# Two ordering edits on ScalarE and VectorE in a fused two-layer kernel: the first join of the slot softmax, and the activation-table switches of the last rounds

## The reference, cut to what matters

```python
# layer 0: s is self-attention with Q = K = V; g is a soft mixture of 64 experts with 32 slots each
logits = (einsum('tzd,ed->tze', x, phi_w) + phi_b).reshape(t, z, 64, 32)
D = softmax(logits, axis=3); C = softmax(logits, axis=2)
X_tilde = einsum('tznp,tzd->npd', D, x)                  # sums over ALL rows
X_tilde = tanh(layernorm(clip(X_tilde, -33000, 65000)))  # eps 1e-5
Y_tilde = einsum('npd,ndH->npH', X_tilde, expert_w) + expert_b[:, None, :]
Y = einsum('tznp,npH->tzH', C, Y_tilde)
# layer 1: s is a gated linear recurrence over each sequence, RMS-normalised; g a token-mixing FFN
log_a = log(sigmoid(lam) + 1e-8); a_t = exp(8 * r_t * log_a)
gated = sqrt(1 - a_t*a_t + 1e-6) * (i_t * x_proj);  h = a*h + gated   # scan over the sequence
```

## Time and profile before

| what | value |
|---|---|
| time, median of 3 runs | 1244.29 us (1239.99 to 1247.22) |
| the profiled execution's own time | 1247.22 us |
| its span, first to last instruction | 1245.2 us |
| PE busy | 1171.4 us, 94% of the span |
| DVE busy | 1096.9 us, 88% |
| POOL busy | 998.5 us, 80% |
| ACT busy | 865.2 us, 69% |
| mean granted TensorE clock | 0.973 |

### The profile page before, as it was taken

How to read it: one execution, slowest core, us unless ns; L and a number is a source line. 1 busy time by engine, 2 the same in 40 slices (tenths; PEclk the granted TensorE clock), 3 DMA queues, 4 the chain that set the end, 5 groups by cost and what they waited for, 6 DMA issues and landing times. The chain is left out here.

```text
span 1245.2 us, 17223 instructions
## 1 busy us (share of the span) xinstructions
PE 1171.4 (94%) x4994; PEld 776.9 (62%) x4994; DVE 1096.9 (88%) x1596; ACT 865.2 (69%) x1930; POOL 998.5 (80%) x804
## 2 busy tenths in 40 slices
PE   6599999999999999999589999999999999999984
PEld 2366666666666666665267777766777776776751
DVE  6989999999999999999457899889989998999863
ACT  2666666666766666666457887877887787787764
POOL 3499999999999999999478787777788777778720
PEclk9799999999999999999789999999999999999997
DMA  6443334443333344334835343434444343444300
GB/s 192 132 150 124 144 135 151 153 152 134 135 132 147 139 152 152 140 140 147 242 107 160 110 153 104 151 110 136 134 129 140 115 135 128 136 135 129 121 32 17
DMA packets 123214, 167.33 MB, mean 134 GB/s; under 512 B 7153, under 2 KB 99313, under 8 KB 122993
## 3 DMA queue, kind: packets, MB, share of 16 engines
q1 hardware_dynamic: 122688, 164.65, 39.3%
q10 hardware_dynamic: 434, 1.59, 0.4%
HBM read 90.71 MB, written 75.50 MB: 133 GB/s over the span
## 5 line engine op out<-in xcount | busy, mean ns | idle before, releaser
L138 POOL TENSOR_TENSOR exp_slots_loaded<-exp_slots_loaded,slot_max 128x1024 f32<-128x1024 f32 x128 | 332.6, 2620 | 59.3 <-DMA exp_slots_loaded<-exp_slots 58.8
L669 POOL TENSOR_TENSOR dd<-ed,rz 128x512 f32<-128x512 f32 x256 | 265.0, 1052 | 23.8 <-ACT rz L560 23.8
L475 PE MATMUL acc<-dd,xns 128*128 128x512 f32 x512 | 262.3, 594 | 2.4 <-POOL dd L669 1.9
L1346 DVE TENSOR_TENSOR clo<-ct,chi 128x512 fp32r<-128x512 f32 x256 | 172.7, 680 | 53.1 <-ACT chi L1187 51.9
L611 DVE TENSOR_REDUCE mr<-lg 128x16 fp32r<-128x512 f32 x256 | 170.8, 688 | 21.1 <-PE lg L442 17.2
L538 ACT ACTIVATE exp_slots_loaded<-lg 128x512 f32<-128x512 f32 x256 | 145.7, 595 | 55.2 <-PE lg L463 51.5
L680 POOL TENSOR_TENSOR ch<-exp_slots_loaded 128x512 f32<-128x512 f32 x128 | 165.5, 1293 | 12.3 <-ACT exp_slots_loaded L538 12.3
L1187 ACT ACTIVATE chi<-ct 128x512 fp32r<-128x512 f32 x256 | 150.2, 594 | 20.4 <-PE ct L935 19.4
L935 PEld LDWEIGHTS ct<-identity,exp_slots_loaded 128*128 128x128 f32 x1024 | 125.1, 142 | 59.5 <-issue 19.5
L935 PE MATMUL ct<-identity,exp_slots_loaded 128*128 128x128 f32 x1024 | 153.1, 275 | 6.3 <-DVE clo L1346 3.3
L463 PE MATMUL lg<-shift_experts_to_slots,mt 128*128 128x512 f32 x256 | 156.6, 651 | 0.5 <-ACT ed L529 0.5
(11 more groups left out here) (186 smaller groups left out, 2443.7 us busy)
## 6 DMA issues: line engine op xcount, KB each, us to landing
exp_slots<-exp_slots_loaded SPq DMA_DIRECT2D x128, 512.0 KB, 2.8
exp_slots_loaded<-exp_slots SPq DMA_DIRECT2D x128, 512.0 KB, 4.1
xns<-xn_rows SPq DMA_DIRECT2D x128, 64.0 KB, 2.5
expert_w<-in_expert_w SPq DMA_DIRECT2D x8, 512.0 KB, 5.2
b_xraw<-in_xT SPq DMA_DIRECT2D x16, 256.0 KB, 3.8
out_t<-b_ti SPq DMA_DIRECT2D x16, 256.0 KB, 2.1
xn_rows<-slot_max SPq DMA_DIRECT2D x2, 1024.0 KB, 5.1
xn_rows<-slot_sum SPq DMA_DIRECT2D x2, 1024.0 KB, 5.2
```

Source lines behind the costliest of these rows:

```text
L138: e.tensor_tensor(rows, rows, joined(SM, b)[:, h].unsqueeze(2).broadcast_to([P, TPB, GC * EPC, NP]), ALU.mult).then_inc(s_we)
L475: e.matmul(acc[k][:, :], xns[v % RX][:, :], dd[v % RX][:, bank(k)], start=tile == 0, stop=tile == NT - 1, skip_group_check=True).then_inc( ...
L669: e.tensor_tensor(dd[v % RX][:, bank(k)].rearrange("q (n p) -> q n p", p=NP), ed[v % RD][:, bank(k)].rearrange("q (n p) -> q n p", p=NP), ...
L1346: e.tensor_tensor(clo[c % RC][:, :], ct[c % 2][:, :], hi_f32(chi[c % RC][:, :]), ALU.subtract).then_inc(c_l)
```

## The change

The diff has two independent parts. In stage 1b, ScalarE's part of the first join moves from behind its second square to the head of its queue, and VectorE's first part of the join moves from ahead of the four centrings to behind them. In stage 2, the two table preloads are guarded with `within(i)` in place of `i >= 0`. As they are called with i - 1, this takes away the calls of rounds 17 and 18 (arguments 16 and 17), four preloads in all, and leaves those of rounds 1 to 16.

```diff
             def scalar1b(e):
+                join_factors(e, 0)
                 for q in range(4):
                     e.wait_ge(s_ce, q + 1)
                     e.activation(sq[:, bank(q)], xc[:, bank(q)], ACT.Square).then_inc(s_sq)
-                    if q == 1:
-                        join_factors(e, 0)
...
             def vector1b(e):
                 for q in range(4):
                     e.tensor_scalar(XTT[:, bank(q)], XTT[:, bank(q)], -33000.0, 65000.0, ALU.max, ALU.min).then_inc(s_cl)
-                join_max(e, 0)
                 for q in range(4):
                     e.wait_ge(s_me, q + 1)
                     e.tensor_tensor(xc[:, bank(q)], XTT[:, bank(q)], pm[q][:, :], ALU.subtract).then_inc(s_ce)
+                join_max(e, 0)
                 join_inverse(e, 0)
...
                 def log_table(i):
-                    if i >= 0:
+                    if within(i):
                         e.preload_act_table_set("natural_log_exp_and_others")
...
                 def tanh_table(i):
-                    if i >= 0:
+                    if within(i):
                         e.preload_act_table_set("exp_and_others")
```

## The result

The changed kernel takes 1253.44 us in the median of 20 runs, against 1243.69 us of 20 runs of the kernel before. The ratio is 1.0078, with a 95% interval of 1.0054 to 1.0102. It is slower by 9.7 us (6.7 to 12.7). The forecast was no change, at 1244.7 us within 1240.5 to 1252.0, so the time lies outside the range. Rival 1, with 1251.6 us, is the case that came true.

A forecast was written before the change was run, and what follows sets the result against it. TensorE was taken as busy for 94% of the span, with dependent chains in stage 1b and the tail. Stage 1b's +1.7 and the tail's -1.3 us gave +0.4 on the 1244.3 us median: 1244.7 us, range 1240.5 to 1252.

The forecast's parts named there:

- Rival 1: Tail: the compiler's set for Ln lacks Exp, so each alternation costs a load; +7.3 us in all, 1251.6 us, chance 0.25.
- Part 2, the inserted loads: Tail: the compiler reinserts the load at input_log(14) in the removed call's place, cost 0; three loads instead of four.
- The gain of 1.30 us: Round 17: the removed Tanh load ahead of deviation_inverse(15) leaves the chain, its replacement lying in idle time; 1.30 us gained.
- Rival 2: Tail: the load for input_tanh(15) goes behind the wait and is paid in full; +1.7 us, 1246.0 us, chance 0.10.
- Part 1, the relay: Stage 1b: maximum after the last centring, factors 2.34 us later, Ln for lam 3.18 us after them, Tanh 2.3 us later.
- Squares and variances: Stage 1b: squares held behind the factors add nothing; variances done at 612.0, 0.9 us before the fourth deviation Ln.
- Part 1, the end of the stage: Stage 1b: its end moves by +1.7 us, as expert weight loads take 3.7 us instead of 4.4; range 0.7 to 2.3.
- The upper bound of 2.3: End of stage 1b: the full 2.3 us delay is paid if the expert weight loads are no quicker.
- Rival 3: Stage 1b: weight bandwidth alone sets the end, so the 2.3 us vanish; -1.3 us, 1243.0 us, chance 0.10.
- The noise: Whole kernel: comparison noise taken as 0.5%, 6.2 us, so no change to be measured.

The follow-up runs named there:

- e10: The kernel before without the one preload at the head of stage 1 (line 570); 1592.47 us in its one execution.
- e3: The kernel before with only the Tanh preload guarded, the call for Ln and Exp kept in rounds 17 and 18; 1242.87 us, ratio 0.9992.
- e7: The kernel before with the lam job ahead of the join on ScalarE and only the Tanh preload guarded; median 1244.77 us, ratio 0.9997.
- e1: The kernel before with only the two join moves in stage 1b, preloads as before; 1249.1 us, ratio 1.0024.
- e11: The changed kernel with the log_table guard put back to i >= 0, so the Ln and Exp call stands in rounds 17 and 18; ratio 0.9993 to before.
- e2: The kernel before with only the two preload guards, join as before; 1251.13 us, ratio 1.0055.
- e6: The kernel before with only round 18's preloads removed; last sequence's Tanh of y to the span's end 42.27 us, 40.06 before.
- e4: The kernel before with only ScalarE's join move; one execution, last centring to Tanh 7.82 us, 8.50 before.
- e5: The kernel before with only VectorE's join move, the maximum behind the centrings; one execution, last centring to Tanh 10.69 us, 8.50 before.

## Why the prediction was wrong, point by point

- **Part 2, the inserted loads.** This is the step that failed. The prediction said that the load for `input_log(14)` "takes the same place", and put it at 0, which takes for granted that it brings the same set. With it went "Exp is also in the set that is active, so nothing has to be loaded there". The place was right, the set was not: behind each Ln without a preload the next Exp got a load too (1.28 us each), and ten loads stood where three were forecast. Rival 1 named the mechanism, its count comes to the ten loads, and it was sized at 3.0 us in round 17 and 2.6 us in round 18. Measured between the two traces: 3.05 and 2.87, T +5.9. It had 0.25. That the sizes came so near is partly luck. In the kernels whose code there is that of before, the first stretch spreads from 17.83 to 19.02 us (seven kernels, mean 18.34) and the second from 20.92 to 22.23 (six, mean 21.40). Against these means the two kernels with ten loads, 22.07 twice and 23.91 and 24.56, are 3.7 and 2.8 us longer. Stage 1 of e10 shows the same: 257 loads, where the kernel before has one. How the compiler chooses the set, no run shows.
- **The gain of 1.30 us** at `tanh_table` of round 17 needed the set with both to be active. Where it was (e3), the gap between Ln and Exp shrank by 1.29 us. The mechanism was right and its condition wasn't met. A switch costs 1.28 us with 0.01 to 0.02 behind it in all these rows.
- **Rival 2** is half right. The load went behind one of the two waits, the one for the output DMA, but not behind the wait for the gate's product (e3), and so it was not paid in full: nothing in e3, 0.7 us in e7. The earlier trace rows were a poor witness. That activation has two waits as well, and nothing shows whether the load at 2.82 stood behind one of them that had ended early.
- **Part 1, the relay.** Factors to Ln for lam took 608.98 - 605.78 = 3.20 us (3.18 expected). The 0.02 us of issue between the last centring and the maximum is shown by no run. In the changed kernel the maximum started at 604.66, 0.09 us ahead of the centring's recorded end (604.06 + 0.69 = 604.75). From the last centring to Tanh it became 2.32 us longer (2.34 expected). Squares and variances set nothing, as worked out: the variances' passes ended at 606.77 + 5.34 = 612.11 and the fourth Ln started at 612.92, 0.8 us later (0.9 expected).
- **Part 1, the end of the stage.** The term of +1.7 was too small for this pair of traces, where A grew by 2.55. The loads were no quicker: 621.70 - 617.44 = 4.26 us for the first (3.7 expected) and 5.09 from the first to the last (4.64). On top, copy to centred took 0.28 us longer (8.01 against 7.73, with a granted clock of 0.50 against 0.80 from 601 to 603 us). The upper bound of 2.3 left that out. (By the span's own clock the end of the splits moved from 627.94 to 628.97 + 1.26 = 630.23, by 2.29, since the stage began 0.26 us earlier.) Over more kernels the term is smaller: A of after, e1 and e11 has the mean 33.78, A of before, e2, e3 and e6, which have the stage 1b of before, 31.76. That is 2.0 us, so 1.7 was near, and 2.55 holds part of the spread between executions.
- **Rival 3** has a core of truth that I hadn't seen: where Tanh came early, TensorE waited for the expert weights (4.35 us in e4, 2.80 in e7), so the DMAs cut gains and not this loss.
- **The noise.** Distances in the traces give 2.55 + 5.92 = 8.5 us. With 20 runs each, 9.7 us (6.7 to 12.7) could be told from nothing, and agrees.

## What to carry to other kernels

The table loads that the program left out here were put in by the compiler, ten in this tail and 257 in stage 1 of e10. What has to be asked is not only whether and where, but which set. Where Ln and Exp alternate, name the set that served both here (natural_log_exp_and_others) at the head of every stretch that can be entered with another one, the tail of a software pipeline included. When a short side job shares queues with the main chain, look at what stands behind its last step: here three steps on one column made a whole relay part of the chain.

## What the runs showed of the hardware

- TensorE's means in stage 1b are the same matmuls in all kernels. In e4 and e5 they ran wholly at a granted clock of 1.00 (eight passes in 3.70 us), in the ten others of the table partly at 0.50 (5.13 us before and 5.40 after). Between e5 and the changed kernel that is worth 1.7 us in copy to centred (6.31 against 8.01). The tail also spreads, 39.16 to 40.23 us for one code.
- Which functions one load served is read from where the next load stands. With natural_log_exp_and_others, stage 1 of the kernel before runs 128 Ln (line 554) and 640 Exp (lines 529, 538 and 560) behind the one load of line 570. With exp_and_others, the Exp at 1218.80 and the Tanh at 1224.16 stand behind the one load at 1217.50. The first doesn't serve Tanh: one load stands at line 801 in the kernel before, one at line 1228 in e3. The second doesn't serve Ln: the changed kernel has a load at line 1257, at 1206.97. No run shows whether another set serves Ln and Tanh.
- Every table load in the lists of the thirteen kernels has a mean of 1283 ns, whether the kernel calls it (line 570) or not (lines 250 and 801 of the kernel before).
- A table load that the compiler put in ran ahead of the activation's only wait at line 1272 (load at 1242.82, activation at 1244.96). At the input gate's Tanh, which has two waits, it ran behind the one for the output DMA (e3, e7, e11: 3.43 to 3.44 us idle ahead of the load) and ahead of the one for TensorE.
- The long middle of stage 2 took from 569.3 to 579.7 us, at a granted clock of 0.99 to 1.00. What makes this spread is open; it is larger than either part of the change.
